# Local attention in a 16-sequence transformer program: the order of a step's work on TensorE, ScalarE and VectorE

## The reference, cut to what matters

```python
# per layer l; 16 sequences, n = 256 tokens, 8 heads of 64, window 64
q, k, v = split(h @ wqkv[l], 3)              # then to heads
q = q / max(norm(q), 1e-12) * q_scale        # the same for k with k_scale
q, k = rotary_xpos(q, k)                     # q*cos*scale + rotate_half(q)*sin*scale; k with 1/scale
sim = (q * 8) @ k.T                          # each window of 64 against itself and the one before
sim = where((i < j) | (i > j + 64) | no_such_key, -big, sim)
o = softmax(sim) @ v
x = x + o @ wo[l]                            # then a gated feed-forward layer
```

## Time and profile before

| | us |
|---|---|
| median of 3 runs | 2302.54 (2301.33 to 2312.95) |
| the profiled execution | 2294.92 |
| its span, first to last instruction | 2293.1 |

### The profile page before, as it was taken

One profiled execution on the slowest core, in us unless ns is written; L12 is line 12 of the kernel. 1 busy time (PEld: TensorE's weight loads), 2 busy tenths in 40 slices (PEclk: granted clock), 3 DMA queues, 4 the chain that ended last, 5 costly groups with the idle time before them and its releaser, 6 DMA issues. The chain is left out here.

```text
span 2293.1 us, 67424 instructions
## 1 busy us (share of the span) xinstructions
PE 2136.7 (93%) x22342; PEld 1585.6 (69%) x22342; DVE 1706.8 (74%) x4362; ACT 1801.0 (79%) x6112; POOL 1431.8 (62%) x1432
## 2 busy tenths in 40 slices
PE   6997999998797999999999999898999999999999
PEld 4994666665795888854888854674788864788863
DVE  5565999996555899964899964675899963899964
ACT  4775999995676999973999973556999982999982
POOL 3663777774662888840888850671788850788850
PEclk8997999999899999999999999999999999999999
DMA  6111000000113000000000000000000000000000
GB/s 249 44 42 42 2 0 0 0 1 38 35 44 111 12 7 9 7 3 3 11 7 9 7 0 0 2 0 6 9 9 8 8 1 5 9 9 7 9 1 37
DMA packets 22568, 46.02 MB, mean 20 GB/s; under 512 B 5344, under 2 KB 13664, under 8 KB 22048
## 3 DMA queue, kind: packets, MB, share of 16 engines
q1 hardware_dynamic: 17440, 34.07, 4.4%
q0 software_dynamic: 4992, 10.23, 1.6%
HBM read 24.51 MB, written 11.40 MB: 16 GB/s over the span
## 5 line engine op out<-in xcount | busy, mean ns | idle before, releaser
L280 POOL TENSOR_TENSOR space<-space 128x512 f32<-128x512 f32 x256 | 325.8, 1273 | 270.4 <-DVE space L383 270.1
L275 POOL TENSOR_TENSOR space<-space 128x512 f32<-128x512 f32 x256 | 267.6, 1045 | 128.1 <-ACT space L316 127.6
L330 ACT ACTIVATE space<-psum,space 128x128 f32<-128x128 f32 x1024 | 337.0, 385 | 2.7 <-DVE space L374 2.7
L177 PE MATMUL psum<-big,space 128*128 128x256 f32 x1024 | 267.9, 384 | 7.3 <-issue 3.5
L269 POOL TENSOR_TENSOR space<-space 128x512 f32<-128x512 f32 x256 | 267.0, 1043 | 7.9 <-DVE space L354 7.3
L1008 POOL TENSOR_TENSOR space<-space 128x256 f32<-128x256 f32 (+1 forms) x256 | 221.9, 888 | 75.2 <-DVE space L1117 70.9
L374 DVE TENSOR_REDUCE space<-psum 128x4 f32<-128x512 f32 x256 | 177.1, 692 | 100.8 <-PE psum L192 96.5
L1053 ACT ACTIVATE space<-space 128x128 f32<-128x128 f32 (+1 forms) x512 | 226.1, 446 | 7.3 <-DVE space L1108 6.5
L330 ACT ACTIVATION_READ_ACCUMULATOR space<-psum,space 128x1 f32 x1024 | 201.8, 197 | 0.0
L177 PEld LDWEIGHTS psum<-big,space 128*128 128x128 f32 x1024 | 175.6, 191 | 29.6 <-issue 16.2
L677 ACT ACTIVATE big<-psum,wt 128x512 f32<-128x512 f32 (+1 forms) x96 | 65.4, 686 | 151.9 <-PE psum L654 151.9
(11 more groups left out here) (194 smaller groups left out, 5425.8 us busy)
## 6 DMA issues: line engine op xcount, KB each, us to landing
big<-early SPq DMA_DIRECT2D x1, 6944.0 KB, 27.9
rows<-space SPq DMA_DIRECT2D x16, 256.0 KB, 2.7
z<-token_y SPq DMA_DIRECT2D x16, 256.0 KB, 4.7
space<-z SPq DMA_DIRECT2D x64, 64.0 KB, 1.9
space<-z SPq DMA_DIRECT2D x64, 63.8 KB, 2.1
big<-late SPq DMA_DIRECT2D x1, 3114.0 KB, 13.7
x<-x_t SPq DMA_DIRECT2D x4, 512.0 KB, 6.0
x_final<-x SPq DMA_DIRECT2D x8, 256.0 KB, 2.0
```

The costliest lines, as they stand in the source:

```text
L177: ins = mm(qk_ps[:, t * T:(t + 1) * T].rearrange("p (n c) -> p n c", n=2), hT[:, k, t * P:(t + 1) * P], wq[:, 0:2, j, :], start=(t == 0), ...
L275: pool.tensor_tensor(x, x, rn[:, (j - 1) % 2, :].unsqueeze(2).to_broadcast([P, 8, LD]), ALU.mult).then_inc(scaled, 1)
L280: pool.tensor_tensor(t3[:, j % 2, :], t1[:, j % 2, :], t2[:, j % 2, :], ALU.add).then_inc(summed, 1)
L330: ins = act.activation(pr[:, j % 2, h, t * P:(t + 1) * P], s_ps[h][:, t * P:(t + 1) * P], ACT.Exp, bias=nm[:, j % 2, h, t:t + 1], accum_ou ...
```

## The change

The four passes keep their instructions and their tiles. The order inside a step changes:

- TensorE: the projection of v and the transposition of q and k come ahead of the transposition of the softmax weights, which is now last. The scores wait for `rl_ready` of the unit before, in addition; one more `compute_val` is made.
- ScalarE: Ln comes between the copies L295 and L301, Exp behind L301 and ahead of the square. They stood behind the square.
- VectorE: the sum of squares comes first, then the mask (which now waits for `p_ready` of the unit before), then the reciprocal. The addition of the output's halves moves from the end of step u + 4 to step u + 5, behind the reciprocal.

```diff
--- before.py
+++ after.py
@@ -162,7 +162,7 @@
     def tensor_body(pe, i, only=None):
         for s, b, k, j in steps(i):
             if not isinstance(s, int):
-                for n in (1, 3, 4):
+                for n in (1, 2, 3, 4):
                     pe.compute_val(S0 + s - n)
             if begins(s, only):
                 pe.wait_ge(h_there[k], H0 + 32 * (i + 1))
@@ -185,6 +185,8 @@
                 pe.wait_ge(g.late_loaded, 16)
                 pe.wait_ge(qk_ready, S0 + u + 1)
                 pe.wait_ge(masked, S0 + u + 1)
+                if at_least(u, 1):
+                    pe.wait_ge(rl_ready, S0 + u)
                 for w, q0, spans in ((0, 0, ((0, 0, WIN),)), (1, LD, ((0, 0, P),)), (0, P, ((P, P, WIN), (P + WIN, WIN, WIN))), (1, P + LD, ((P, P, P),))):
                     for col, k0, n in spans:
                         for h in range(2):
@@ -220,6 +222,28 @@
                     pe.wait_ge(z_ready, B0 + b - 1)
                 mm(z_ps, wo[:, c, :], oT[:, (j - 5) % 2, :], start=(c == 0), stop=(c == CH - 1), skip_group_check=True).then_inc(wo_ready, 1)
 
+            if runs(s, U):
+                if is_first(s):
+                    prev.free(pe, 2)
+                if at_least(s, 1):
+                    pe.wait_ge(v_ready, S0 + s)
+                if at_least(s, 4):
+                    pe.wait_ge(o0_ready, S0 + s - 3)
+                for t in range(2):
+                    ins = mm(v_ps[:, t * P:(t + 1) * P], hT[:, k, t * P:(t + 1) * P], wq[:, 2, j, :], start=(t == 0), stop=(t == 1), skip_group_check=True)
+                ins.then_inc(vp_ready, 1)
+
+            u = s - 1
+            if runs(u, U):
+                pe.wait_ge(scaled, S0 + u + 1)
+                if is_first(u):
+                    prev.free(pe, 1)
+                if at_least(u, 1):
+                    pe.wait_ge(qk_ready, S0 + u)
+                for n in range(2):
+                    for t in range(2):
+                        ins = nc.tensor.transpose(qkT_ps[:, n * T + t * P:n * T + (t + 1) * P], t3[:, (j - 1) % 2, t * T + n * P:t * T + (n + 1) * P], g.ident32)
+                ins.then_inc(turned, 1)
             u = s - 3
             if runs(u, U):
                 pe.wait_ge(normed, S0 + u + 1)
@@ -231,29 +255,6 @@
                     for t in range(2):
                         ins = nc.tensor.transpose(pt_ps[:, h * T + t * P:h * T + (t + 1) * P], pr[:, (j - 3) % 2, h, t * P:(t + 1) * P], g.ident32)
                 ins.then_inc(ptp_ready, 1)
-
-            if runs(s, U):
-                if is_first(s):
-                    prev.free(pe, 2)
-                if at_least(s, 1):
-                    pe.wait_ge(v_ready, S0 + s)
-                if at_least(s, 4):
-                    pe.wait_ge(o0_ready, S0 + s - 3)
-                for t in range(2):
-                    ins = mm(v_ps[:, t * P:(t + 1) * P], hT[:, k, t * P:(t + 1) * P], wq[:, 2, j, :], start=(t == 0), stop=(t == 1), skip_group_check=True)
-                ins.then_inc(vp_ready, 1)
-
-            u = s - 1
-            if runs(u, U):
-                pe.wait_ge(scaled, S0 + u + 1)
-                if is_first(u):
-                    prev.free(pe, 1)
-                if at_least(u, 1):
-                    pe.wait_ge(qk_ready, S0 + u)
-                for n in range(2):
-                    for t in range(2):
-                        ins = nc.tensor.transpose(qkT_ps[:, n * T + t * P:n * T + (t + 1) * P], t3[:, (j - 1) % 2, t * T + n * P:t * T + (n + 1) * P], g.ident32)
-                ins.then_inc(turned, 1)
             others("tensor", pe, s)
 
     def tensor(pe):
@@ -293,12 +294,22 @@
                 if at_least(u, 2):
                     act.wait_ge(s_ready, S0 + u - 1)
                 act.activation(qk[:, j % 2, :], qkT_ps, ACT.Copy).then_inc(qk_ready, 1)
+            u = s - 1
+            if only is None and runs(u, U):
+                act.wait_ge(ss_ready, S0 + u + 1)
+                act.activation(lnn[:, (j - 1) % 2, :], ss[:, (j - 1) % 2, :], ACT.Ln, scale=float(2 ** 20), bias=g.tiny[:, 0:1]).then_inc(ln_ready, 1)
             u = s - 4
             if only is None and runs(u, U):
                 act.wait_ge(ptp_ready, S0 + u + 1)
                 if at_least(u, 2):
                     act.wait_ge(ol_ready, S0 + u - 1)
                 act.activation(pt[:, j % 2, :, :].rearrange("p h n -> p (h n)"), pt_ps, ACT.Copy).then_inc(pt_ready, 1)
+            u = s - 1
+            if only is None and runs(u, U):
+                act.wait_ge(ln_ready, S0 + u + 1)
+                if at_least(u, 2):
+                    act.wait_ge(scaled, S0 + u - 1)
+                act.activation(rn[:, (j - 1) % 2, :], lnn[:, (j - 1) % 2, :], ACT.Exp, scale=-0.5, bias=g.tiny[:, 1:2]).then_inc(rn_ready, 1)
             if begins(s, only):
                 act.wait_ge(proj_ready, S0 + s + 1)
                 if at_least(s, 2):
@@ -306,14 +317,6 @@
                 act.activation(sq[:, j % 2, :], qk_ps, ACT.Square).then_inc(sq_ready, 1)
             if only is not None:
                 continue
-            u = s - 1
-            if runs(u, U):
-                act.wait_ge(ss_ready, S0 + u + 1)
-                act.activation(lnn[:, (j - 1) % 2, :], ss[:, (j - 1) % 2, :], ACT.Ln, scale=float(2 ** 20), bias=g.tiny[:, 0:1]).then_inc(ln_ready, 1)
-                act.wait_ge(ln_ready, S0 + u + 1)
-                if at_least(u, 2):
-                    act.wait_ge(scaled, S0 + u - 1)
-                act.activation(rn[:, (j - 1) % 2, :], lnn[:, (j - 1) % 2, :], ACT.Exp, scale=-0.5, bias=g.tiny[:, 1:2]).then_inc(rn_ready, 1)
             u = s - 4
             if runs(u, U):
                 act.wait_ge(ol_ready, S0 + u + 1)
@@ -346,24 +349,32 @@
 
     def vector_body(dve, i, only=None):
         for s, b, k, j in steps(i):
+            u = s - 1
+            if only is None and runs(u, U):
+                dve.wait_ge(sq_ready, S0 + u + 1)
+                if at_least(u, 2):
+                    dve.wait_ge(ln_ready, S0 + u - 1)
+                dve.tensor_reduce(ss[:, (j - 1) % 2, :], sq[:, (j - 1) % 2, :].rearrange("p (m d) -> p m d", m=8), AX.X, ALU.add).then_inc(ss_ready, 1)
+            u = s - 2
+            if only is None and runs(u, U):
+                if is_first(u):
+                    prev.free(dve, 3)
+                    prev.free(dve, 4)
+                if at_least(u, 1):
+                    dve.wait_ge(p_ready, S0 + u)
+                dve.tensor_copy(s_pair, band).then_inc(masked, 1)
             u = s - 3
             if only is None and runs(u, U):
                 dve.wait_ge(p_ready, S0 + u + 1)
                 if at_least(u, 2):
                     dve.wait_ge(normed, S0 + u - 1)
                 dve.reciprocal(rl[:, (j - 3) % 2, :, :], ls).then_inc(rl_ready, 1)
-            u = s - 2
+            u = s - 5
             if only is None and runs(u, U):
-                if is_first(u):
-                    prev.free(dve, 3)
-                    prev.free(dve, 4)
-                dve.tensor_copy(s_pair, band).then_inc(masked, 1)
-            u = s - 1
-            if only is None and runs(u, U):
-                dve.wait_ge(sq_ready, S0 + u + 1)
+                dve.wait_ge(o0_ready, S0 + u + 1)
                 if at_least(u, 2):
-                    dve.wait_ge(ln_ready, S0 + u - 1)
-                dve.tensor_reduce(ss[:, (j - 1) % 2, :], sq[:, (j - 1) % 2, :].rearrange("p (m d) -> p m d", m=8), AX.X, ALU.add).then_inc(ss_ready, 1)
+                    dve.wait_ge(wo_ready, S0 + u - 1)
+                dve.tensor_tensor(oT[:, (j - 5) % 2, :], ol[1], o0[:, (j - 5) % 2, :], ALU.add).then_inc(o_ready, 1)
             if only is None and j == 1 and runs(b - 2, B):
                 dve.wait_ge(wo_ready, S0 + CH * (b - 1))
                 z = tokens(g.z, b - 2)
@@ -383,12 +394,6 @@
                 dve.tensor_tensor(halves(t2[:, j % 2, :]), halves(qk_ps)[:, :, ::-1, :], halves(tab[:, 1, :]), ALU.mult).then_inc(rotated, 1)
             if only is not None:
                 continue
-            u = s - 4
-            if runs(u, U):
-                dve.wait_ge(o0_ready, S0 + u + 1)
-                if at_least(u, 2):
-                    dve.wait_ge(wo_ready, S0 + u - 1)
-                dve.tensor_tensor(oT[:, j % 2, :], ol[1], o0[:, j % 2, :], ALU.add).then_inc(o_ready, 1)
             others("vector", dve, s)
 
     def vector(dve):
```

More of the change, by code:

```diff
@@ L221, in tensor_body @@
                 mm(z_ps, wo[:, c, :], oT[:, (j - 5) % 2, :], start=(c == 0), stop=(c == CH - 1), skip_group_check=True).then_inc(wo_ready, 1)
-            u = s - 3
-            if runs(u, U):
-                pe.wait_ge(normed, S0 + u + 1)
-                if is_first(u):
-                    prev.free(pe, 5)
-                if at_least(u, 1):
-                    pe.wait_ge(pt_ready, S0 + u)
-                for h in range(2):
-                    for t in range(2):
```

(13 more changed lines are left out.)

## The result

The changed kernel took 2321.66 us (median of 4 runs, 2318.58 to 2326.83) where the kernel before took 2303.85 beside it: ratio 1.0072, 95% interval 1.0039 to 1.0106. A second comparison gave 1.0062 (1.0044 to 1.0080). So it is slower by 14 to 18 us; the forecast was no difference, 2302. The profiled execution took 2321.76 us, its span is 2320.0. Of the 26.9 us between the two spans some 10 are not the change's: the first Exp of the first pass started at 749.9 us instead of 739.6, behind stages that the change does not touch; in the profiles of the other kernels here, which differ in local attention alone, that start lies between 721 and 751, and near together for kernels measured in one group (721 to 729, 744 to 746, 748 to 751).

A forecast was written before the change was run, and what follows sets the result against it. A loop over ScalarE, GpSimd and TensorE (3.96 us) bounds an ordinary step; VectorE's ring at 3.98 replaces it, and extras make the mean 4.02 against 4.023. Forecast 2302 us, its own range 2292 to 2311.

The forecast's parts named there:

- The hop from the reciprocal to the scores: From VectorE's reciprocal end to TensorE's first score matmul: 0.11 us, bounds 0.05 and 0.16.
- VectorE's ring: Maximum through sum of squares, mask and reciprocal to the scores and back: 3.98 us, setting the changed kernel's step.
- v's wait with its weights: On TensorE, v loses 0.03 us waiting for the output copy and 0.05 for weights not fetched ahead.
- TensorE's own turn: Sum of TensorE's pitches over one step: becomes 3.93 us, bounds 3.85 and 3.95.
- extras: Loop's end 0.24 us and turn of a batch 0.08 us in eight steps, raising the mean from 3.98 to 4.02.
- The old ring: Loop over ScalarE, GpSimd and TensorE setting the step before: 3.96 us, falling to 3.36 and binding no more.
- L366 in L391's place: On VectorE, the sum of squares, 0.58 us, enters the ring where the output's L391, at most 0.42, stood.
- GpSimd without slack: GpSimd's L269 and L275, 1.05 us each, end about when the q/k transposition is due: free, without slack.
- Rival A: ScalarE's ring over the outputs, with Ln added, sets the step at 4.02 to 4.08 us; about 2320 us; chance 0.29.
- Rival B: Neither VectorE's nor ScalarE's ring binds; TensorE's turn of 3.85 to 3.93 us is left; about 2281 us; chance 0.23.
- The most contended engine is to be optimized first: Skill's rule: the engine with highest occupancy comes first; the prediction set it against VectorE's ring, third in occupancy.

The follow-up runs named there:

- half_squares: Changed kernel with the sum of squares over half of each head's elements, the rest left out: mean step 4.048 us, 1.0034 times the kernel before.
- weights_split: Changed kernel with the softmax weights' transposition split, first head ahead of v, second last: mean step 4.063 us, 1.0063 times the kernel before.
- v_behind_qk: Changed kernel with the projection of v moved behind the transposition of q and k: mean step 4.200 us, 1.0241 times the kernel before.
- weights_split_half: Changed kernel with the weights' transposition split around v and q/k, and half of the squares left out: mean step 3.947 us, 0.9920 times the kernel before.
- split_rec_first: Changed kernel with the weights' transposition split, reciprocal ahead of the mask, scores on two waits: mean step 4.022 us, 1.0012 times the kernel before.

## Why the prediction was wrong, by its steps

Two terms failed. The hop from the reciprocal to the scores was put at 0.11 and measured 0.17, so that VectorE's ring is 4.05 and not 3.98. And v's wait with its weights was put at 0.08 and measured 0.20, so that TensorE's own turn is 4.05 and not 3.93. Either alone holds the step at 4.05, as half_squares (4.048) and weights_split (4.063) show, and with both taken away it falls to 3.947. The forecast mean was 3.98 + 0.04 for extras = 4.02; measured is 4.05 + 0.01 = 4.06.

- *The old ring binds, and the change dissolves it.* Right: 3.96 then, no wait of L245 or L276 now.
- *VectorE's ring takes over at 3.98.* The ring was right in its instructions. The hop was mis-sized: 0.11 for what measured 0.17 in the changed kernel, 0.18 in weights_split, and 0.15 behind the mask with two waits. I took it from ScalarE's copy to the output matmuls, which give 0.10 and not 0.11. Its upper bound, 0.16, was nearer. The ring is 4.05, but it does not take over alone.
- *TensorE's own turn becomes 3.93, at most 3.95.* This failed, and the bound with it: 4.05. The sum for v had four terms, each a little short: L211 0.70 for 0.68, its end to the copy 0.06 for 0.03, the copy 0.38 for 0.36, its end to v 0.14 for 0.05 to 0.11; v itself lost 0.08 for 0.05. No row stood behind the 0.03: where that copy waited for the output matmuls in the kernel before, it started 0.05 behind them at the earliest. Added on a path that was due to the hundredth (1.12 to 1.18 against 1.14), that is 0.12 in the wait and 0.08 in v, 0.20 in place of 0.08.
- *Extras of a batch and a loop, 0.04 a step.* They are 0.01 (4.062 less 4.05), where they were 0.055 before. That slack in the rings takes them is a reading and was not tested. The miss in this term hid 0.03 of the miss in the two others; that is luck.
- *L366 in L391's place is what costs.* Right for VectorE's ring; it did not decide alone, as half_squares shows.
- *GpSimd without slack.* Right as a warning: v_behind_qk turned it into 4.20 with one move.
- *Rival A* named the right size (4.02 to 4.08 a step, about 2320 us), by another cause; its own ring is 3.95. That the measured time lies at its figure is chance. *Rival B* needed both rings short; weights_split_half shows that even then 3.95 is left and not 3.85.
- *The most contended engine is to be optimized first* (the Trainium skill, Perfetto Trace Analysis, Identifying the Most-Contended Engine). The trace does not bear this out here: ScalarE's busy time fell from 214.80 to 205.73 of 220 us and the step grew by 0.04. The ring decided, not the occupancy.

Summed over the four passes, first Exp to last, the kernel before takes 1011.5 us and the changed one 1022.7 and 1023.0 in its two profiles: the steps explain 11 of the 14 to 18 us. The stretches between and behind the passes are another 5.3 and 3.1 longer. Their cause was not shown: from the last Exp of one pass to the first of the next, 91 to 93 us go by in profiles of one and the same kernel.

## What to carry to other kernels

When a loop over engines is near saturation, list every ring through it, those that close only after two turns too, and sum each; removing the longest is worth no more than its distance to the second. Work that lies in a wait is free, and moving it out of there can put its length on a ring. If two rings have one length, each edit alone shows nothing: try them together before either is called innocent. And do not carry a hop over from another wait: the hops onto TensorE here ran from 0.06 to 0.18 us, and a forecast that rests on a few hundredths needs the hop of the very wait, or its upper bound.

## What the runs showed of the hardware that was not expected

- The hop from a result to TensorE's first matmul that waits for it has no single value: 0.06 us from GpSimd's end to L255, 0.10 from a ScalarE copy's end to the output matmuls (weights_split_half), 0.14 from a ScalarE copy's end to v (the changed kernel), 0.15 from the mask's end to the scores with two waits (split_rec_first), and 0.26 from the mask's end with a third wait, for the reciprocal, behind it (weights_split).
- The first matmul behind such a wait also costs more: in the changed kernel v takes 0.52 us to the next instruction where q/k and weights, of the same shape and without a wait, take 0.43 to 0.44.
- A ScalarE copy of 128x512 is recorded with 0.65 where it starts 0.17 before its predecessor's recorded end (L296 of the changed kernel), and with 0.59 where it starts 0.10 before it (L301 in the earlier trace rows; L296 of v_behind_qk). The next instruction starts 0.47 to 0.50 later either way. So a recorded duration depends on the predecessor.
